# Wider products for T, an earlier p, and a moved store of column sums in a cross-attention kernel

## The reference

```python
g_x = _conv1x1(g_w, g_b, x_2).transpose(0, 2, 1)
theta_x = _conv1x1(theta_w, theta_b, x).transpose(0, 2, 1)
phi_x = _conv1x1(phi_w, phi_b, x_2)
W = jnp.einsum('bnc,bcm->bnm', theta_x, phi_x) / phi_x.shape[-1]
y = jnp.einsum('bnm,bmc->bnc', W, g_x).transpose(0, 2, 1)
wy = _conv1x1(w_w, w_b, y)
inv_std = jax.lax.rsqrt(bn_var + EPS)
wy = bn_gamma[None, :, None] * (wy - bn_mean[None, :, None]) * inv_std[None, :, None] + bn_beta[None, :, None]
return wy + x
```

## Time and profile before

| | us |
|---|---|
| median of 3 runs | 749.16 |
| lowest and highest run | 749.09 and 749.34 |
| the profiled execution | 749.25 |
| its span, first to last instruction | 747.4 |

### The profile page before, as it was taken

The page is one execution under the profiler, slowest core; times in us unless marked ns, Lnnn a source line. Parts: engine busy times, 40 slices in busy tenths (PEclk is TensorE's granted clock), DMA queues, the critical chain, the costliest instruction groups (busy, mean ns, idle before and its releaser), DMA issues.

```text
span 747.4 us, 12831 instructions
## 1 busy us (share of the span) xinstructions
PE 739.8 (99%) x3795; PEld 637.0 (85%) x3795; DVE 584.3 (78%) x1296; ACT 489.9 (66%) x1341; POOL 334.9 (45%) x239
## 2 busy tenths in 40 slices
PE   7999999999999999999999999999999999999998
PEld 6687988889888888888889888888888889888886
DVE  3887878868787787888868788787887868788685
ACT  4666775766857576775766857576775767857441
POOL 5947152462615527163462615527163462615500
PEclk9999999999999999999999999999999999999999
DMA  9927466182754709366182653708356182650202
GB/s 271 197 104 171 181 114 240 40 211 102 149 203 79 252 20 229 122 112 239 33 215 103 142 209 74 245 32 219 132 112 239 28 213 110 133 219 9 119 1 114
DMA packets 89980, 107.18 MB, mean 143 GB/s; under 512 B 4426, under 2 KB 70884, under 8 KB 89956
## 3 DMA queue, kind: packets, MB, share of 16 engines
q1 hardware_dynamic: 87824, 105.83, 49.1%
q10 hardware_dynamic: 2132, 1.05, 0.7%
HBM read 73.28 MB, written 33.59 MB: 143 GB/s over the span
## 4 chain that ended last, share of the span: by engine, by line
PE 97%; DMA 1%; DVE 1%; ACT 0%; POOL 0%; issue 0%; ACTq 0%; DVEq 0%
PE wbank L913 50%; PE gbank L913 46%; PE wbank L959 1%; DMA ctx_sb<-in_ctx_dram 1%; PE wbank L937 0%; PE wbank L965 0%; DVE gbank L875 0%; DVE th_lo L811 0%; ACT room L472 0%; POOL ctxT_lo L379 0%; PE wbank L949 0%; DVE ctxT L655 0%; ACT th_hi L601 0%; PE wbank L1090 0%; ACT ctxT_hi L449 0%
## 5 line engine op out<-in xcount | busy, mean ns | idle before, releaser
L379 POOL TENSOR_TENSOR ctxT_lo<-ctxT,ctxT_hi 128x512 fp32r<-128x512 f32 x124 | 160.4, 1319 | 286.8 <-ACT ctxT_hi L449 286.8
L424 POOL TENSOR_TENSOR x_lo<-x_sb,x_hi 128x1024 fp32r<-128x1024 f32 x60 | 142.5, 2407 | 0.0
L564 ACT ACTIVATE mt<-stage 32x224 fp32r<-32x224 f32 (+1 forms) x210 | 70.2, 334 | 98.0 <-DVE stage L701 93.6
L903 DVE SCALAR_TENSOR_TENSOR x_sb<-wbank,const,x_sb 128x512 f32<-128x512 f32 x110 | 77.5, 747 | 69.6 <-PE wbank L913 69.6
L472 ACT ACTIVATE room<-ctx_sb 128x256 f32<-128x256 f32 x240 | 96.3, 403 | 21.1 <-issue 21.1
L913 PE MATMUL gbank<-ctxT_lo,ctxT_hi 128*128 128x512 f32 x360 | 84.0, 389 | 0.0
L913 PE MATMUL gbank<-z_hi,mt 128*128 128x512 f32 x256 | 81.6, 390 | 0.0
L655 DVE STREAM_TRANSPOSE ctxT<-ctx_sb 128x512 f32<-128x512 f32 x124 | 78.7, 683 | 2.6 <-DMA ctx_sb<-in_ctx_dram 2.6
L913 PE MATMUL wbank<-x_hi,wt_hi 128*128 128x512 f32 x256 | 79.6, 392 | 0.0
L913 PEld LDWEIGHTS gbank<-ctxT_lo,ctxT_hi 128*128 128x128 f32 x360 | 67.6, 188 | 14.0
L913 PE MATMUL wbank<-x_lo,wt_hi 128*128 128x512 f32 x256 | 79.0, 390 | 0.0
(11 more groups left out here) (137 smaller groups left out, 1528.0 us busy)
## 6 DMA issues: line engine op xcount, KB each, us to landing
x_sb<-in_x_dram SPq DMA_DIRECT2D x16, 2048.0 KB, 7.8
out_dram<-x_sb SPq DMA_DIRECT2D x63, 512.0 KB, 4.7
ctx_sb<-in_ctx_dram SPq DMA_DIRECT2D x124, 256.0 KB, 4.6
s_row<-s_dram SPq DMA_DIRECT2D x15, 256.0 KB, 3.5
ctx_sb<-in_ctx_dram ACTq DMA_DIRECT2D x4, 256.0 KB, 7.2
x_sb<-in_L_xattn_w_w_dram SPq DMA_DIRECT2D x1, 512.0 KB, 9.2
stage<-in_L_xattn_theta_w_dram SPq DMA_DIRECT2D x1, 512.0 KB, 14.6
phi_nat<-in_L_xattn_phi_w_dram SPq DMA_DIRECT2D x1, 512.0 KB, 13.7
```

The source lines that it names most:

```text
L379: nc.gpsimd.tensor_tensor(ctxT_lo[:, c, :], turned_ctx(b, c), f(ctxT_hi[:, c, :]), ALU.subtract).then_inc(sem_, 1)
L424: nc.gpsimd.tensor_tensor(x_lo[:, k, :], x_sb[par][:, k, :], f(x_hi[:, k, :]), ALU.subtract).then_inc(x_lo_made, 1)
L564: return nc.scalar.activation(dst, src, ACT.Copy)
L903: nc.vector.scalar_tensor_tensor(out=x_sb[par][:, m, cols], in0=OUT_BANK[m][h][:, :], scalar=const[:, m:m + 1], in1=x_sb[par][:, m, cols], ...
```

## The change

Three edits, which share two semaphores and the banks:

1. **T.** `wp_hi` and `wp_lo` become the two halves of one tile `wp`, so that one matmul of 512 columns makes high by high in columns 0 to 255 and high by low in columns 256 to 511 of a bank; the low part by `wp_hi` stays a matmul of 256 columns into columns 0 to 255. Each block has a bank of its own: `gbank` 0, `wbank` 3, 1, 2 (batch 0: `gbank` 0, 1, 2, `wbank` 1). DVE adds the two halves: the addition of the bias term is followed by a second instruction that adds columns 256 to 511. PE now waits for `th_lo` of theta(0) ahead of blocks 2 and 3, whose banks held theta(0), and no longer for the evacuation of T blocks.
2. **p.** From batch 2 on, p of batch b+1 is made in batch b, ahead of DVE's evacuation of out's last row.
3. **s_dram.** SP writes the column sums between the two halves of the context's loads. For batch 1 alone, ACT's and POOL's parts of the sums stand elsewhere.

```diff
-    T_BANK = [0, 1, 2, 0]
-        wp_hi = sb("wp_hi", [P, KC, CI], F32R)
-        wp_lo = sb("wp_lo", [P, KC, CI], F32R)
+        wp = sb("wp", [P, KC, 2 * CI], F32R)
+        wp_hi, wp_lo = wp[:, :, 0:CI], wp[:, :, CI:2 * CI]
+        FIRST_T_BANK = [gbank[0], gbank[1], gbank[2], wbank[1]]
+        T_BANK = [gbank[0], wbank[3], wbank[1], wbank[2]]
...
                     load_ctx(b + 2, 0)
-                    sp.wait_ge(ctxT_made, CH * b + 2 * CH)
-                    load_ctx(b + 2, 1)
                 if nxt:
                     sp.wait_ge(whole_made, b + 1)
...
                     sp.dma_start(s_dram.rearrange("(q k) -> q k", q=32), whole_sum[0:32, :]).then_inc(s_written, 16)
+                if nxt2:
+                    sp.wait_ge(ctxT_made, CH * b + 2 * CH)
+                    load_ctx(b + 2, 1)
+                if nxt:
                     sp.wait_ge(s_written, 16 * b + 16)
...
-                                                   in1=gbank[T_BANK[r]][:, 0:CI],
-                                                   op0=ALU.mult, op1=ALU.add).then_inc(t_taken, 1)
+                                                   in1=t_bank(b, r)[:, 0:CI],
+                                                   op0=ALU.mult, op1=ALU.add).then_inc(t_half, 1)
+                    dve.wait_ge(t_half, KC * b + (r + 1))
+                    nc.vector.tensor_tensor(stage[:, r * CI:(r + 1) * CI], stage[:, r * CI:(r + 1) * CI],
+                                            t_bank(b, r)[:, CI:2 * CI], ALU.add).then_inc(t_taken, 1)
...
+                def make_p(b):
+                    if not first(b):
+                        dve.wait_ge(in_s, 16 * b)
+                        dve.wait_ge(q_taken, KI * b)
+                        dve.wait_ge(s_taken, b)
...
+                if first(b) or second(b):
+                    make_p(b)
...
                 for m in range(KC):
+                    if m == KC - 1 and nxt and not first(b):
+                        make_p(b + 1)
...
-                        mm(dst, g_h, wp_hi[:, j, :], n == 0, False)
-                        mm(dst, g_h, wp_lo[:, j, :], False, False)
-                        ins = mm(dst, g_l, wp_hi[:, j, :], False, n == KC - 1)
+                        mm(dst[:, :], g_h, wp[:, j, :], n == 0, False)
+                        ins = mm(dst[:, 0:CI], g_l, wp_hi[:, j, :], False, n == KC - 1)
...
                 t_block(0)
+                t_block(1)
+                if not first(b):
+                    pe.wait_ge(th_lo_made, NT * b + 1)
+                t_block(2)
...
-                pe.wait_ge(t_taken, KC * b + 1)
+                pe.wait_ge(th_lo_made, NT * b + (1 if first(b) else NH))
                 t_block(3)
```

More of the change, by code:

```diff
@@ L291, in first, with t_bank, second @@
             return isinstance(b, int) and b == 0
+        def t_bank(b, r):
+            return FIRST_T_BANK[r] if first(b) else T_BANK[r]
+        def second(b):
+            return isinstance(b, int) and b == 1
         def batches(eng, body):
@@ L413, in prep_ctx @@
                 for c in range(CH):
-                    if c == RING:
+                    if c == RING and not second(b):
                         add_halves(b)
-                    if c == RING + 2:
+                    if c == RING + 2 and not second(b):
                         add_folded(b)
@@ L422, in prep_x @@
                 for k in range(KC):
+                    if k == 0 and second(b):
+                        add_halves(b)
+                    if k == KC - 1 and second(b):
+                        add_folded(b)
                     pool.wait_ge(x_hi_made, KC * b + (k + 1))
@@ L619, in body @@
                     hi(q_hi[:, k, :], gbank[Q_BANK[k]][:, :], q_hi_made)
+                if nxt and not first(b):
+                    fold_half(b + 1)
+                theta(1)
                 if first(b):
@@ L629, in body @@
                     prep_x(b + 1, half + (1 if par else 0), 1 - par)
+                    if first(b):
+                        fold_half(1)
                     sum_columns(b + 1)
@@ L847, in body @@
                     chain(nc.vector.tensor_scalar(nbp_col[:, :], bp_col[:, :], float(N), None, ALU.mult))
[L848 to L856, removed]
+                def make_p(b):
[3 more added lines that the diff above has]
+                        dve.wait_ge(s_taken, b)
+                    for k in range(KI):
+                        row = S_BANK[:, :].rearrange("p (k q) -> p k q", q=32) if first(b) else s_row_by_channel
+                        nc.vector.tensor_tensor_reduce(junk[:, k, :].rearrange("p (k q) -> p k q", q=32), row,
+                                                       phi_nat[:, k, :].rearrange("p (k q) -> p k q", q=32), 1.0, 0.0,
+                                                       ALU.mult, ALU.add, p1_raw[:, k:k + 1]).then_inc(s_made, 1)
+                    dve.wait_ge(s_made, KI * b + (KC + KI))
+                    nc.vector.tensor_tensor(p1[:, :], p1_raw[:, :], nbp_col[:, :], ALU.add).then_inc(s_taken, 1)
+                if first(b) or second(b):
+                    make_p(b)
                 if first(b):
@@ L1069, in t_block @@
                     m = T_ORDER[r]
-                    dst = gbank[T_BANK[r]][:, 0:CI]
+                    dst = t_bank(b, r)
                     order = sorted(range(KC), key=lambda j: (j, m) not in HELD)
@@ L1106, in body @@
                     theta(1, (0, 1))
-                pe.wait_ge(t_taken, KC * b + 3)
+                if first(b):
+                    pe.wait_ge(t_taken, 3)
                 for r, j in enumerate(T_ORDER):
```

6 lines of the change are left out of this document (1 added, 5 removed).

## The result

The changed kernel takes 789.25 us (median; 788.94 to 789.75), the kernel before 749.25 on the same chip. The ratio is 1.0532, with a 95% interval from 1.0519 to 1.0544: 40 us slower. The profiled run took 789.75, its span is 787.9 and the mean granted clock 0.998. The clock is at full (2.4 GHz) through the span but for 3.41 us in batch 1, where it is at half; that counts in batch 1 and nowhere else. The other three runs have means of 0.995 to 0.998.

What follows compares the result with a forecast made beforehand. PE's stream was taken to set the time. Waits of 44.9 us (35.7 at gram and T, 9.1 at out, 0.1 in batch 1) less T's 3.4 gave +41.5 on 749.25, 790.7 us; range 757 to 803.

Steps and rivals of the forecast that it cites:

- p ahead of out's last row: On DVE, p's two-SBUF-input products and POOL's `x_lo` block each other in turns; row 3 is 4.65 us late.
- Both rivals on it: For p's products beside POOL: no block, 747.2 us, 20%; or blocked once, not twice, 758.4 us, 8%.
- That correction: At row 3: PE's wait ahead of out moves row 3's due time but not `x_lo`; lateness 4.95 becomes 4.65 us.
- Who waits for it: PE, at the gram rows and T behind late DVE: 2.55 us a batch, in batches 2 to 15.
- The slack of 1.14 + 0.97: DVE's idle before the gram turns (1.14 us) plus PE's margin on `gram_lo` before T (0.97), taken off row 3's lateness.
- The ACT chain into out: Late T evacuation delays ACT's sums and `q_hi`; PE waits 0.7 us at `out_part(0, 1)` in batches 2 to 14.
- T's products: On PE in T, a block falls from 1.440 to 1.387 us; 0.21 saved a batch, 3.4 us for 16 batches.
- The lower bound (0): T's saving could be 0 if a pair of different widths pays more than in either row; upper bound 3.4 us.
- Which batches pay: Batches 2 to 15 pay 2.55 us each, batches 2 to 14 also 0.7, batch 1 pays 0.1.
- The sums' store: On SP's queue the store moves between the load halves, to about 373.4; `s_row` lands near 383.0 (382.5 to 385).
- Nothing on the path: The store's move was to delay nothing PE needs: x comes some 5 us later, needed 30 us after.
- the DMA has no say: If `s_row` came late, the fourth `x_lo` would go first and both products still end at the same 389.

Runs made afterwards that it cites:

- e1: Changed kernel with p back in its old place behind T's last low part: 756.23 us, ratio 1.0095 to the kernel before.
- e2: Changed kernel with p still early, but its product reading a PSUM bank in place of `s_row`: 757.0 us, ratio 1.0100 to the kernel before.
- e3: Changed kernel with POOL's third `x_lo` waiting until p is made: 757.12 us, ratio 1.0107 to the kernel before.
- e5: Kernel before with T's products, banks and evacuation alone changed: 750.71 us, ratio 1.0014.
- e8: Kernel before with T's change and batch 1's moved sums, `whole_sum` behind the first `x_lo`; p and loads as before: 749.40 us, ratio 1.0004.
- e11: T's change and moved sums, p and loads as before, with 512-column products in batches 2 to 13 and 15 alone: 747.64 us, 0.9977 to the kernel before.
- e4: Changed kernel with batch 1's column sums added on ACT and POOL where they were, ahead of `x_lo`: 783.67 us, ratio 1.0457 to the kernel before.
- e9: Changed kernel with the column sums' store back behind both halves of the context's loads: 786.20 us, ratio 1.0498 to the kernel before.
- e6: Kernel before with p alone made ahead of out's last row: 787.75 us, ratio 1.0514.

## Why the prediction was right

It gave 790.7 us and the time is 789.25. The mechanism is the one it named, but several of its terms were off, and they nearly cancel.

**p ahead of out's last row.** Right, and shown three ways (e1, e2, e3). Both rivals on it are out: the product does block, and it blocks twice. Row 3 is 4.15 us late, not 4.65. The turns went in the forecast's order and a little faster: the products end 0.85 and 0.84 behind an `x_lo` (forecast 0.91), and from the end of the third `x_lo` to row 3 it is 4.05 us (forecast 4.33). Their start was off too. The third `x_lo` ended 0.59 us past the batch's first matmul in the forecast's rows and does so 0.08 past it now, since PE's own waits move row 3's due time and not `x_lo`. That correction was set at 0.3 and is 0.5. Each of the two makes about half of the difference.

**Who waits for it.** The slack of 1.14 + 0.97 was right. 4.15 − 2.11 is 2.04, and the stages gram, theta and T of the table, less T's saving, show 1.73 + 0.23 + 0.11 = 2.07. The forecast's 2.55 was this with the other lateness.

**The ACT chain into out.** Forecast 0.7, measured 0.03 + 0.10 + 0.39 = 0.5 in Q, theta(1) and out.

**T's products.** The mechanism was right and the size was not. A pair takes 0.353 us, not 0.347: blocks come every 1.41 (382.22, 383.73, 385.15, the first with a wait of 0.1). The stage is 5.64 long without that wait (e1) instead of 5.55, and saves 0.11 a batch, not 0.21. Two matmuls among their own kind pay 2 × 0.0133 beyond their columns; a pair of different widths pays 0.033. The lower bound (0) had named this case. (The range's upper end, 803, was worked out with the full 3.4 saved; with the bound of 0 it would have been 807.) The wait that the longer evacuation was to cost, 0.1 a batch, is absent in the loop (e1: out 10.88 as before) and is 0.5 to 0.6 in the two batches outside it (e5, e8, e11).

**Which batches pay.** Batch 15 was charged 2.55 and pays nothing: it has no next context, so DVE's stream behind p is shorter by four turns (in the trace the gram turns follow row 3 at 745.22), and its time from the first gram matmul to the end is 0.1 less than before. This was to be seen in the order.

**The sums' store.** "Nothing on the path" failed in batch 1. The forecast followed the queue of batch 7, where `whole_sum` is ready when the first half of the loads is out. In batch 1 the change makes `whole_sum` behind three `x_lo`, and the store's wait for it holds four loads. Each of the two edits is free there without the other (e4 and e9 both bring batch 1 to 45.49); together they cost 7.1 of the 7.7 us, some 1.5 of it through the half clock behind PE's stands. The other 0.5 is T's change (e11). The prediction took batches 0 and 1 as ±1 us, without a row of batch 1's queue. In the loop, "the DMA has no say" holds to 0.3 us (e9), which the earlier store saves.

In all: +2.5 a batch for 12 batches (forecast 3.0), +2.8 in batch 2, +7.7 in batch 1 (forecast 0), 0 in batch 15 (forecast +2.3). Over the batches the forecast was 9.1 us too high in 2 to 15 (6.5 in batches 3 to 14, 0.2 in batch 2, 2.4 in batch 15) and 8.2 too low in 0 and 1. That it came within 1.5 us of the time is luck: the direction and most of the 40 us were forecast from a mechanism that held, but two errors of 8 and 9 us cancel.

## What to carry to other kernels

Before an instruction is moved into an idle slot, look at what the other engines do in that slot. Idle on DVE is no room for an instruction with two SBUF inputs while POOL streams through SBUF: give it one input in PSUM, or let POOL stand until it is done. And when a transfer is moved ahead of another in one queue, look at when its data is ready in every batch, those written out ahead of the loop first of all, for it holds all behind it.

## What the hardware showed that was not expected

- The same product takes 1.05 us with both inputs in SBUF and 0.69 with one in PSUM, read with the same stride (e2: 686 ns in the mean, beside a busy POOL). A plain subtraction of 512 columns takes 0.69 with both in SBUF, so it is this kind of instruction that pays, and where the price lies inside it stays open.
- DVE and POOL take turns by whole instructions: in batch 7 the waiting side went next all three times, and each was held for as long as the other's instruction ran. In e8 this makes a DVE instruction of 0.42 us into one of 1.59 or of 0.47, by 0.14 us of phase.
- Matmuls of 512 and of 256 columns in turn take 0.353 us a pair, 6 ns more than one of each in rows of their own kind (0.2267 + 0.120). Why is open.
- Why batch 0 is 1.4 to 1.6 us longer with T's change and the old sums (e4, e5) was traced to ACT's order only; which of T's edits makes it tight there was not tried. Both runs have the full clock there.
- PE's stands can cost twice. In batch 1 of the changed kernel the granted clock falls from 1.0 to 0.5 for 3.41 us behind stands of 3.3 and 2.3 us, and T's pairs take 0.64 us there and not 0.35. No run here shows that the stands cause it: in e6's profiled run it falls behind stands of 1.74 and 1.77 us in batches 6 and 7, and not behind stands of much the same length in its other batches.
